# A fused transformer layer on one Trainium2 core: other instruction orders for the last attention

## What is computed

```
h = _rms(x, w_ln1)
q = (h @ wq + bq).reshape(B, S, N_HEADS, HEAD_DIM)      # k, v alike; then rope on q and k
scores = jnp.einsum('bqhd,bkhd->bhqk', q, k) * HEAD_DIM ** (-0.5)
scores = jnp.where(causal[None, None], scores, jnp.finfo(scores.dtype).min)
attn = jax.nn.softmax(scores, axis=-1)
ctx = jnp.einsum('bhqk,bkhd->bqhd', attn, v)
x = x + ctx @ wo
h = _rms(x, w_ln2); logits = h @ w_router; top 2 of 8 experts of width 352
sh = jax.nn.silu(h @ w_sh_gate) * (h @ w_sh_up) @ w_sh_down     # a shared expert of width 1408
```

## Time and profile before

| | |
|---|---|
| median of three runs | 1896.81 us (1896.38 to 1898.08) |
| the profiled execution | 1897.27 us |
| its span, first to last instruction | 1895.4 us |
| TensorE busy | 1530.6 us, 81% |
| VectorE busy | 1183.1 us, 62% |
| ScalarE busy | 888.1 us, 47% |
| GpSimd busy | 810.3 us, 43% |
| the last attention, from its first scores to its last weigh | 1065.6 to 1197 us of the span |

### The profile page before, as it was taken

How to read it: one execution, slowest core, us unless ns; L and a number is a source line. 1 busy time by engine, 2 the same in 40 slices (tenths; PEclk the granted TensorE clock), 3 DMA queues, 4 the chain that set the end, 5 groups by cost and what they waited for, 6 DMA issues and landing times.

```text
span 1895.4 us, 26612 instructions
## 1 busy us (share of the span) xinstructions
PE 1530.6 (81%) x9104; PEld 1167.9 (62%) x9104; DVE 1183.1 (62%) x1731; ACT 888.1 (47%) x1974; POOL 810.3 (43%) x809
## 2 busy tenths in 40 slices
PE   5255877777967777957777799879999999999994
PEld 2134544555645555635556566668788899999973
DVE  4689658987568887489873444343332556565545
ACT  4443345664456664366652366212111566666510
POOL 0586135653145542266532321114431455555544
PEclk8555886888977888958887899989999999999997
DMA  5620000110100111001103200562220676777464
GB/s 192 244 75 26 23 6 25 60 51 28 46 17 34 51 46 31 27 23 51 45 29 117 89 29 29 195 233 83 99 85 1 223 270 234 269 236 267 151 232 160
DMA packets 94486, 195.74 MB, mean 103 GB/s; under 512 B 8769, under 2 KB 25665, under 8 KB 91025
## 3 DMA queue, kind: packets, MB, share of 16 engines
q1 hardware_dynamic: 89232, 177.26, 27.0%
q0 software_dynamic: 5120, 16.78, 2.6%
HBM read 140.40 MB, written 53.61 MB: 102 GB/s over the span
## 4 chain that ended last, share of the span: by engine, by line
PE 42%; issue 5%; DVE 5%; POOL 3%; ACT 2%; DMA 0%; DVEq 0%; ACTq 0%; SPq 0%; POOLq 0%
PE scores L588 20%; PE bank L588 12%; PE bank L770 2%; POOL yab L2162 2%; PE scores L707 2%; PE bank L720 1%; PE bank L652 1%; PE bank L735 1%; DVE YA L1552 1%; PE bank L960 1%; DVE HS L1542 1%; PE scores L710 1%; ACT PT L1180 1%; ACT bank L1137 1%; POOL lal L2155 1%
## 5 line engine op out<-in xcount | busy, mean ns | idle before, releaser
L1996 POOL TENSOR_TENSOR GB<-DU,BB 128x512 f32<-128x512 f32 x256 | 327.6, 1292 | 125.7 <-DVE HS L1542 67.6
L652 PE MATMUL bank<-ident,HS 128*128 128x128 f32 x896 | 184.9, 342 | 172.9 <-DVE YA L1552 118.0
L1542 DVE TENSOR_TENSOR_SCAN HS<-bank,GB 128x512 f32<-128x512 f32 x224 | 273.0, 1219 | 47.6 <-ACT bank L1137 23.9
L652 PEld LDWEIGHTS bank<-ident,HS 128*128 128x128 f32 x896 | 125.0, 172 | 222.3 <-DVE YA L1552 157.1
L1137 ACT ACTIVATE bank<-DL,aneg 128x512 f32<-128x512 f32 x224 | 154.9, 692 | 131.5 <-DVE HS L1542 130.2
L1552 DVE SCALAR_TENSOR_TENSOR YA<-bank,Ct,YA 128x512 f32<-128x512 f32 x224 | 164.3, 733 | 28.6 <-PE bank L652 26.5
L1180 ACT ACTIVATE PT<-bank 128x128 f32<-128x128 f32 (+3 forms) x256 | 110.5, 432 | 128.6 <-PE bank L720 125.9
L588 PE MATMUL scores<-xth,wgh 128*128 128x256 f32 x552 | 158.0, 286 | 2.0 <-DVE fa L1878 1.1
L588 PE MATMUL scores<-xth,wgl 128*128 128x256 f32 x552 | 156.1, 283 | 0.0
L588 PE MATMUL scores<-xtl,wgh 128*128 128x256 f32 x552 | 156.0, 283 | 0.0
L720 PE MATMUL bank<-ident,EX 128*128 128x128 f32 x640 | 129.8, 303 | 27.9 <-ACT PT L1180 25.8
(11 more groups left out here) (272 smaller groups left out, 3697.0 us busy)
## 6 DMA issues: line engine op xcount, KB each, us to landing
wgr<-wffn_in SPq DMA_DIRECT2D x108, 384.0 KB, 6.4
wdr<-wffn_in SPq DMA_DIRECT2D x81, 256.0 KB, 2.9
BB<-b_scratch SPq DMA_DIRECT2D x64, 256.0 KB, 3.2
xg<-V SPq DMA_DIRECT2D x1, 11776.0 KB, 40.2
xr<-xg SPq DMA_DIRECT2D x23, 512.0 KB, 5.7
yg<-ysb SPq DMA_DIRECT2D x23, 512.0 KB, 6.3
hah<-hhd SPq DMA_DIRECT2D x5, 1024.0 KB, 5.7
hal<-hhd SPq DMA_DIRECT2D x5, 1024.0 KB, 8.7
```

The source lines that it names most:

```text
L652: mm = nc.tensor.transpose(state_bank(s, q)[:, et * P:(et + 1) * P], HS[:, n % 2, et, tt * P:(tt + 1) * P], ident[:])
L1542: nc.vector.tensor_tensor_scan(HS[:, n % 2, et, :], decay_bank(s, k), GB[:, k % 4, :], 0.0, ALU.mult, ALU.add).then_inc(scan_done, 1)
L1996: nc.gpsimd.tensor_tensor(GB[:, k % 4, :], DU[:, et, :], BB[:, n % 2, :], ALU.mult).then_inc(gb_ready, 1)
```

## The change

In each of the four engines' blocks the one loop is replaced by two functions, `units` for rounds with both parts and `last_units` for the last attention; the state-space part of round 0 gets a short loop of its own. `units` and that loop issue what the old loop issued, in the same order. `last_units` issues the same instructions as before in another order. SP's list is not touched. The core of the diff, with the loops that are left out marked:

```diff
+            def last_units(b):                       # TensorE
+                for q in range(-1, NQ):
+                    i, m = quad(q)
+                    if q + 1 < NQ:
+                        scores(b, q + 1)
+                    for a in range(HG):
+                        if q > 0:
+                            next(shared)
+                        if q >= 0 and a < HG - 1:
+                            turn(b, HG * q + a + 1)
+                        if q >= 0 and i and (m, a) in ((0, 1), (2, 1), (3, 2)):
+                            finish(b, i - 1, (0, 0, 1, 2)[m])
+                    if q + 1 < NQ:
+                        turn(b, HG * (q + 1))
+                    if q >= 0:
+                        weigh(b, q)
...
+            def last_units(b):                       # ScalarE
+                for a in range(HG):
+                    probs(b, a)
+                for q in range(NQ):
+                    i, m = quad(q)
+                    v, w = HG * q, HG * (q + 1)
+                    more = q + 1 < NQ
+                    if i and m == 1:
+                        finish(b, i - 1, 1)
+                    keep_turned(b, v)
+                    if q:
+                        keep_inverse(b, q - 1)
+                    for n in range(SE):
+                        if up_end(n)[0] + 1 == q:
+                            early_round(n)
+                    if q:
+                        context(b, q - 1)
+                    keep_turned(b, v + 1)
+                    if i and m == 1:
+                        finish(b, i - 1, 2)
+                    if more:
+                        probs(b, w)
+                    keep_turned(b, v + 2)
+                    if more:
+                        probs(b, w + 1)
+                    for n in range(SE):
+                        if gate_end(n)[0] == q:
+                            early_tanh(n)
+                    keep_turned(b, v + 3)
+                    if more:
+                        probs(b, w + 2)
+                        probs(b, w + 3)
+                    if i and m == 2:
+                        finish(b, i - 1, 3)
+                    if m == 3 and more:
+                        finish(b, i, 0)
+                keep_inverse(b, NQ - 1)
+                context(b, NQ - 1)
+                early_round(SE - 1)
...
+            def last_units(b):                       # VectorE
+                row_max(b, 0)
+                for q in range(NQ):
+                    i, m = quad(q)
+                    more = q + 1 < NQ
+                    invert(b, q)
+                    if q:
+                        context(b, q - 1)
+                    if more:
+                        row_max(b, q + 1)
...
```

More of the change, by code:

```diff
@@ L869, in round_ @@
                     rotate(b, 7)
[L870 to L885, removed]
+                if att and scn:
+                    units(b, s)
+                elif scn:
+                    for q in range(NB):
+                        turn_states(s, q)
+                else:
+                    last_units(b)
                 if scn:
-                    for q in range(NB - T4, NB):
-                        turn_states(s, q)
                     for tt in range(T4):
@@ L1289, in round_ @@
                     decay(s, 0)
[L1290 to L1341, removed]
+                if att and scn:
+                    units(b, s)
+                elif scn:
+                    for k in range(1, NB):
+                        decay(s, k)
+                        if k % 8 == 0 and k <= 8 * KC:
+                            round_weights(k // 8 - 1)
+                else:
+                    last_units(b)
@@ L2063, in early_rest, with units, last_units @@
                                         ).then_inc(f_al, 1)
+            def units(b, s):
+                driven(s, 0)
+                driven(s, 1)
+                for q in range(NQ):
+                    i, m = quad(q)
+                    k = T4 * q + 2
+                    if i and m == 1:
+                        finish(b, i - 1, 0)
+                    if i and m == 3:
+                        finish(b, i - 1, 1)
+                    driven(s, k)
+                    driven(s, k + 1)
+                    widen(b, q)
+                    if q:
+                        context(b, q - 1)
+                    if q + 1 < NQ:
+                        driven(s, k + 2)
+                        driven(s, k + 3)
+                context(b, NQ - 1)
+            def last_units(b):
+                for q in range(NQ):
+                    i, m = quad(q)
+                    if i and m == 1:
+                        finish(b, i - 1, 0)
+                    if i and m == 3:
+                        finish(b, i - 1, 1)
+                    widen(b, q)
+                    if q:
+                        context(b, q - 1)
+                    if q == 0:
+                        low_down(0)
+                    for n in range(SE):
+                        if up_end(n)[0] + (up_end(n)[1] > 1) == q:
+                            early_rest(n)
+                context(b, NQ - 1)
+                early_rest(SE - 1)
             def round_(b, s):
@@ L2078, in round_ @@
                             low_gate_up(0)(m - 4)
[L2079 to L2110 removed]
+                if att and scn:
+                    units(b, s)
+                elif scn:
+                    for k in range(NB):
+                        driven(s, k)
+                        if k % 8 == 1 and 1 <= k // 8 <= KC:
+                            rest_weights(k // 8 - 1)
+                else:
+                    last_units(b)
             def low_gate_up(job):
```

168 lines of the change are left out of this document (97 added, 71 removed).

## The result

| | before | after |
|---|---|---|
| median of ten runs each | 1897.76 us | 1892.91 us (1890.82 to 1896.71) |
| ratio after to before, 95% interval | | 0.9973 (0.9963 to 0.9984) |
| profiled execution | 1897.27 us | 1893.44 us |
| its span | 1895.4 us | 1891.7 us |

The changed kernel is 4.85 us faster. The forecast was 1893.0 with a range of 1887.5 to 1899.0. In what follows all executions count but one, which took 4909.02 us beside seven of the same kernel (TensorE's new order alone) at 1889.88 to 1893.97.

The account below looks back on a forecast made before the run. TensorE was taken to set the pace, waiting only for ScalarE's copies in its holes. Waits removed, 13.7 us, less 7.0 for tanh and 2.9 for the row maximum, net 3.8: profiled 1893.5, forecast 1893.0, range 1887.5 to 1899.0.

Parts of the forecast that it names:

- L731's wait: In TensorE's last attention, weigh's wait for ScalarE's last copy (8.4 us) falls under 1; 0.62 to 0.93 saved per step.
- Steps 0 and 15: First and last attention steps, before weigh: 0.4 us saved without pieces, 0.8 us by the fourth piece filling the hole.
- Tanh: Ahead of the fourth turning's copy in steps 1, 3, 5, 7, 12, 14: waits for the piece, adding 7.0 us.
- Rival 4: Tanh costs nothing, the piece ending before ScalarE finishes the exponential ahead: 10.8 us less, 1886.0; chance 0.13.
- Late copies and the maximum: Turnings' waits for late copies shrink by 1.1 us; the row maximum delays exponentials and copies, adding 2.9 us.
- the scores that were to wait 0.2 us behind the exponentials in steps 3 and 7: Exponentials behind tanh were to end 0.2 us after weigh, making the scores wait; part of the 2.9 us added.
- The net of the attention: Last attention: 13.7 us of waits removed, 7.0 and 2.9 us added, leaving 3.8 us less.
- ctl: TensorE's product waiting for POOL's ctl: of 2.2 us only 1.7 behind the last weigh stays, saving 0.5 us.
- The clock: Granted clock in the attention: 1.00 throughout today; six new holes of 0.83 to 1.4 us, no low-clock spell put in.
- The second rival: Clock falls behind every tanh in six steps, 1.7 us each: 6.4 us more, 1903.2; chance 0.05.
- Rival 3: ScalarE becomes the bound, the maximum's end pushing all exponentials: 10 us in place of 2.9, 1900.1; chance 0.12.
- I see no place that gives it back: Behind the attention, engines wait for counts TensorE's chain raises, so the whole 3.8 us goes through to the time.

Follow-up runs that it names:

- the first experiment: Changed kernel with ScalarE's tanh of the early gate moved back to the end of its step: 1886.45 us, ratio 0.9935; run again, 1886.99 us.
- the exponentials spread over the other cover: Kernel before with each TensorE piece behind its turning, plus ScalarE's second exponential behind the third copy and third behind the fourth: 1887.48 us, ratio 0.9935.

## Why the prediction was right, point by point

- **L731's wait goes**: right. It was 8.4 us in 16 times and is in no list of the kernel after. At start to start a plain step at 128, 256 and 384 columns gained 0.56, 0.67 and 0.83 us (steps 2, 6 and 10), where 0.62, 0.72 and 0.83 were counted. From turning to weigh it now takes 0.11 to 0.24, 0.24, 0.36 and 0.46 us at the four widths; the 0.03, 0.16, 0.24 and 0.38 in the prediction were some 0.1 too small.
- **Steps 0 and 15**: too low. They gained 0.57 and 1.15 us, counted as 0.4 and 0.8. Step 0 ran at a granted clock of 0.50 before and after, which the sum did not look at.
- **Tanh**: right in mechanism and close in size. 7.05 us in six steps, shown by the first experiment, against 7.0; less the 0.5 that steps 4 and 15 give back, 6.6 of the attention. The six waits of the turning are 0.94, 0.95, 1.05, 1.05, 1.27 and 1.26 us. Rival 4 (the piece ends before ScalarE is free) falls with it: ScalarE waited for the piece at tanh in all six.
- **Late copies and the maximum**: right for steps 7 and 11, for which 0.45 and 0.8 us were counted and 0.41 and 0.71 measured. Wrong for step 13, whose 0.4 was put down to the maximum as well: with the maximum cut short the step stayed within 0.05 and its turning still waited 0.43. Wrong too for the scores that were to wait 0.2 us behind the exponentials in steps 3 and 7: in the kernel after the scores wait for exponentials once, in step 0. Waits of turnings for late copies other than tanh's are 0.23, 0.28, 0.33, 0.69 and 0.47 us in steps 5, 7, 9, 11 and 13, 2.0 together, next to 2.45 counted for these five steps. So the size of 2.9 is a little too high, and one of its five causes was another.
- **The net of the attention**: 3.8 us less predicted, 4.75 measured. The first experiment splits it: without the tanh the attention is 11.4 us shorter than before, where 13.7 - 2.9 = 10.8 were counted, and the tanh takes 6.6 and not 7.0. Steps 0 and 15 make up 0.5 of the first difference. Steps 4 and 8 gained 1.21 and 1.24 us, more than their 0.72 and 0.83 for weigh; a part of the 0.5 for ctl lies there, and the rest was not looked into.
- **ctl**: right, one wait of 1.7 us is left of 2.2.
- **The clock**: right that none of the six holes would bring a spell, though "1.00 throughout today" leaves out steps 0 and 1, which ran at 0.50 in both kernels. The second rival, a clock that falls behind every tanh, was a guess of mine that no row showed, with its price worked out from the spell of 3.8 us at 0.55: 1.7, where the output products were 1.56 longer. In the kernel after the trace does not bear it out, with 1.00 over 112.5 us and the holes of steps 3 to 14, up to 1.27, in it. In the kernel with TensorE's order alone there is one spell, 0.59 for 3.9 us, and no second one up to the end of the attention. Rival 3 (ScalarE the bound) did not come in the kernel after.
- **Where the prediction was wrong** is its step "I see no place that gives it back" together with the silence on what may come as a gift. The stretch behind the attention was 1.3 us shorter since the low-clock spell of the earlier trace rows did not follow, and that is luck: the wait in front of it is the same 1.69 us, and of the ten profiled executions a spell followed it in two. The experts' part was 1.65 us longer. The two nearly cancel and neither stood in the sum. That 1893.0 came so close to 1892.91 is in part chance: the medians of ten runs differ by 4.85 us, not by 3.8, and before's own median lay 0.95 higher in the larger set of runs, which makes up for it.

**What stays open**: the length of the experts' part, 678.3 to 681.9 us in ten profiled executions of kernels that have the same instructions there. Low-clock spells may account for some of it: between 1400 and 1500 us the kernel after has one (0.83 over 1460 to 1470) where the kernel before has none. But the low-clock time summed over the part, some 37 us before, 47 after and 39 in the first experiment (twice what the clock of each window lacks to 1.00, times its length, in windows of 0.5 us), does not follow its length (678.3, 679.9 and 681.0), so something else moves it too, and no run was made to find out what. The intervals of the ratios have this in them, which is why the experiments were judged by their attention.

## What to carry to other kernels

A copy out of the only bank of a chain of transposes has a turnaround of some 1.3 us at 512 columns (1.31 from the start of the turning to that of weigh), and TensorE must have other work between each turning and whatever needs its copy; which work it is (the next turning, or a piece of something else) did not matter here, within 0.3 us over the attention. Before several engines are reordered it is worth trying one alone: two lines on TensorE gave 11.1 us of the attention, the change on three engines 4.75. When the order of an in-order engine is changed, look for the instruction that waits for a producer which the same change moves behind: a tanh that reads the piece beside it cost 1.2 us a time in front of a copy, and at the step's end 0.5 us in six steps together. And read gains from start to start by step: the column of idle times went from 10.9 to 9.9 us here while the stretch became 4.75 us shorter.

## What the hardware showed that I had not expected

- The same wait of 1.7 us behind the last weigh was followed by a low clock in the kernel before (0.55 for 3.8 us) and not in the kernel after (1.00). Of all ten profiled executions, in which this wait lasts 1.69 us each time, one more has a spell right behind it, that of the exponentials spread over the other cover (0.50 over 1189.6 to 1193.0). A hole's length alone does not tell whether a spell follows.
- Nor does the kernel. The first experiment's kernel was profiled twice: once the clock was 0.51 from 1198.7 to 1205.6, and once it was 1.00 there and 0.50 from 1206.0 to 1209.4, though the two lie only 0.6 us apart in time. A single profile therefore doesn't show that a change brought a spell or took one away.
- With 1.37 us in front of a finish part the clock fell to 0.59 in the kernel with TensorE's order alone; with 1.26 and 1.27 us and a turning and weigh behind them it stayed at 1.00 in the kernel after. The length and the neighbours differ at once, and each kernel has one profile, so the runs don't say what made the difference.
